# One-hots for the edge counts of a two-layer graph network: three targets in one VectorE pass, and a narrower first matmul per tile

## The reference

```python
x = layernorm(x + L0(x, edges))   # x1 = relu(x @ W_ah + b), three attention convolutions of 4 heads, W_out
x = layernorm(x + L1(x, edges))   # two attention convolutions, 4 heads of 512 and one of 768
# one convolution:
h = x @ W;  e = leaky_relu(as_n[src] + ad_n[dst], 0.2)
p = exp(e - segment_max(e, dst)[dst])
out = segment_sum((p / segment_sum(p, dst)[dst])[:, None] * h[src], dst) + b
```

## Time and profile before

| | us |
|---|---|
| median of 3 runs | 1948.07 |
| lowest, highest run | 1946.56, 1950.36 |
| the profiled execution, its own time | 1945.85 |
| span of its trace | 1944.2 |
| outside the span (own time less span) | 1.65 |
| first stage, to the next stage's first matmul | 240.88 |

### The profile page before, as it was taken

How to read it: one execution, slowest core, us unless ns; L and a number is a source line. 1 busy time by engine, 2 the same in 40 slices (tenths; PEclk the granted TensorE clock), 3 DMA queues, 4 the chain that set the end, 5 groups by cost and what they waited for, 6 DMA issues and landing times. The chain is left out here.

```text
span 1944.2 us, 30898 instructions
## 1 busy us (share of the span) xinstructions
PE 1848.0 (95%) x11497; PEld 1783.2 (92%) x11497; DVE 1445.9 (74%) x2468; ACT 1033.4 (53%) x1634; POOL 140.8 (7%) x139
## 2 busy tenths in 40 slices
PE   6999899999999999997999999989999999999998
PEld 5777789998999999997999899989999999999998
DVE  7787669998889988983545549557888886356766
ACT  4666622126798898874211232257788875232633
POOL 5011022111000000000011111100000000000000
PEclk9999989999999999998999999999999999999999
DMA  4122144455284444537654476482342406545302
GB/s 125 53 61 67 27 143 124 124 137 137 72 203 103 106 105 102 134 71 188 191 172 143 134 197 184 132 224 75 113 141 66 138 27 179 168 122 129 101 17 80
DMA packets 179273, 234.13 MB, mean 120 GB/s; under 512 B 75943, under 2 KB 151655, under 8 KB 178889
## 3 DMA queue, kind: packets, MB, share of 16 engines
q1 hardware_dynamic: 170407, 202.98, 38.6%
q0 software_dynamic: 7984, 27.24, 4.8%
q10 hardware_dynamic: 748, 2.10, 0.4%
HBM read 167.27 MB, written 65.00 MB: 119 GB/s over the span
## 5 line engine op out<-in xcount | busy, mean ns | idle before, releaser
L1692 PE MATMUL p_o<-p_hi,h_parts 125*128 125x416 f32 (+1 forms) x960 | 282.6, 355 | 8.8 <-DVE z L1611 6.2
L1118 PE MATMUL p_o<-first_room,p 125*125 125x193 f32 x1200 | 201.7, 329 | 5.7 <-ACT res L1000 2.9
L1118 PEld LDWEIGHTS p_o<-first_room,p 125*125 125x125 f32 x1200 | 197.0, 189 | 7.1 <-issue 6.7
L1118 PE MATMUL p_o<-h_in,p 125*125 125x193 f32 x1200 | 199.8, 329 | 2.8 <-ACT res L1000 2.8
L1118 PEld LDWEIGHTS p_o<-h_in,p 125*125 125x125 f32 x1200 | 197.6, 189 | 4.3 <-issue 3.0
L1692 PEld LDWEIGHTS p_o<-p_hi,h_parts 125*128 125x128 f32 x960 | 181.6, 189 | 14.9 <-DVE z L1611 10.2
L761 DVE CUSTOM_DVE_ANT_0 max_junk<-src_row,G 125x1250 bf16<-125x1250 f32 x120 | 184.9, 1612 | 3.2 <-ACT src_row L799 1.6
L865 PE MATMUL p_h<-pw_hi,x1T 128*125 128x384 f32 x720 | 187.1, 341 | 0.0
L1068 DVE TENSOR_TENSOR e<-e 125x1250 f32<-125x1250 f32 x120 | 174.3, 1452 | 17.2 <-ACT e L1030 17.1
L1073 DVE SCALAR_TENSOR_TENSOR p<-e,CT 125x1250 f32<-125x1250 f32 x120 | 175.3, 1461 | 4.6 <-PE p_o L1118 0.4
L1408 PE MATMUL p_h<-pw_hi,x2T 128*125 128x256 f32 (+1 forms) x960 | 173.7, 283 | 0.0
(11 more groups left out here) (270 smaller groups left out, 3920.0 us busy)
## 6 DMA issues: line engine op xcount, KB each, us to landing
f_raw<-turned SPq DMA_DIRECT2D x40, 500.0 KB, 9.0
h_parts<-h_rows SPq DMA_DIRECT2D x40, 448.0 KB
turned<-tail_room SPq DMA_DIRECT2D x18, 625.0 KB, 7.3
G<-turned SPq DMA_DIRECT2D x20, 562.5 KB
h_rows<-tail_room SPq DMA_DIRECT2D x22, 424.4 KB
h_rows<-h_out SPq DMA_DIRECT2D x16, 560.0 KB
h_rows<-tail_room SPq DMA_DIRECT2D x14, 560.0 KB
first_room<-in_w_gat POOLq DMA_DIRECT2D x36, 192.0 KB, 2.7
```

Source lines behind the costliest of these rows:

```text
L1118: last = nc.tensor.matmul(p_o[:, b, n * 256:n * 256 + C0 + 1], p[:, g % RING, d * T:(d + 1) * T], h_in[hh][:, s, 0:C0 + 1], start=(s == 0 ...
L1692: last = nc.tensor.matmul(p_o[:, bank(n, c), 0:w], h[:, s, kind, cols].bitcast(F32R), pp[:, g % RING, 0:w], start=(s == 0 and j == 0), sto ...
```

## The change

VectorE makes the target one-hots of slots 0, 1 and 2 by one `tensor_tensor` over 3 x 125 columns: `node_no` repeated three times against the three edge targets, each repeated 125 times (these are F32, `node_no` is I16, the output BF16). The wait ahead of it is for slot 2's buffers of the run before; slots 0 to 2 of `src_hot` then have no wait of their own, slot 3 keeps its own. ScalarE makes the target one-hot of slot 3 alone, so `apart` has one buffer. TensorE opens each bank with the diagonal's columns alone, which lie in one bank or two (126 in all, with an even start and width), and a bank without any of them with two columns; the slice of `band` is now at a constant place.

```diff
-        BY_DVE = RUN // 2
+        BY_DVE = RUN - 1
...
             def one_hots(t, first, count, before):
                 with dve.Fori(0, count) as j:
+                    at = bass.ds(first + j, 1)
+                    dve.wait_ge(hot_free, (before + j) * RUN + BY_DVE)
+                    v.tensor_tensor(dst_hot[:, 0:BY_DVE, :],
+                                    node_no[:, bass.ds(t * T, T)].rearrange("p (o n) -> p o n", o=1).broadcast_to([T, BY_DVE, T]),
+                                    edge_col[:, 1, 0:BY_DVE, at].broadcast_to([T, BY_DVE, T]), ALU.is_equal)
                     for h in range(RUN):
-
-                        dve.wait_ge(hot_free, (before + j) * RUN + (h + 1))
-                        at = bass.ds(first + j, 1)
-                        hot = v.tensor_scalar(src_hot[:, h, :], node_no[:], edge_col[:, 0, h, at], None, ALU.is_equal)
-                        if h < BY_DVE:
-                            hot = v.tensor_scalar(dst_hot[:, h, :], node_no[:, bass.ds(t * T, T)], edge_col[:, 1, h, at],
-                                                  None, ALU.is_equal)
-                        hot.then_inc(hot_ready, 1)
+                        if h >= BY_DVE:
+                            dve.wait_ge(hot_free, (before + j) * RUN + (h + 1))
+                        v.tensor_scalar(src_hot[:, h, :], node_no[:], edge_col[:, 0, h, at], None, ALU.is_equal).then_inc(hot_ready, 1)
...
                 for i, (a, w) in enumerate(CH):
-                    nc.tensor.matmul(p_count[:, i, 0:w], ident_b, band[:, bass.ds(t * -T + (N - T + a), w)],
+                    lo, hi = max(a, t * T), min(a + w, (t + 1) * T)
+                    lo, hi = (lo - a - (lo - a) % 2, hi - a + (hi - a) % 2) if lo < hi else (0, 2)
+                    nc.tensor.matmul(p_count[:, i, lo:hi], ident_b, band[:, N - T + a + lo - t * T:N - T + a + hi - t * T],
                                      start=True, stop=False, skip_group_check=True)
```

## The result

| | before | after |
|---|---|---|
| median, us | 1948.88 (4 runs, 1946.56 to 1950.36) | 1965.6 (4 runs, 1962.13 to 1969.5) |
| ratio after / before | | 1.0094, 95% interval 1.0077 to 1.0112 |
| profiled execution, its span | 1944.2 | 1960.4 |
| first matmul of the next stage | 240.88 | 260.23 |

The kernel became 16.7 us slower; 22.4 had been forecast. The first stage lost 19.35 us, and the later stages took 3 less in this execution.

The account below looks back on a forecast made before the run. TensorE was taken to bound the first stage, with VectorE level; 27.0 - 3.4 - 1.4 + 1.2 - 1.0 = +22.4 us gave a median of 1970.5. Forecast proper 1964 to 1977 (0.70), wider range 1960 to 1981 (about 0.83).

Parts of the forecast that it names:

- The added wait and its row: Between count runs, TensorE waits for VectorE's pass and a source one-hot: 3.05 us a run against 2.15, 0.90 more.
- Thirty passages: Run-to-run passages that pay 0.90 us: 19 in tiles 1 to 4, 6 and 8, 11 in tiles 5, 7, 9; +27.0 us.
- what ScalarE gives back: ScalarE's wait moves to slot 3: 0.57 us in six tiles, -3.4; the late tiles 5, 7, 9 gain 0.47 each, -1.4.
- the free first passage: In tiles 1 to 4, 6 and 8 the first passage costs nothing, as TensorE waits for ScalarE in the first run anyway.
- the four paid ones: In tile 5 VectorE itself comes late, so every passage counts: four at 0.90 us.
- The opening at nothing: Narrower opening of each tile costed at nothing, covered by waits for ScalarE or VectorE; uncovered it would be 2.2 us.
- The end of a tile: The low part of x, on which turn_x waits, comes 0.3 us later in tiles 2, 4, 6 and 8: +1.2 us.
- Tile 0: GpSimd holds VectorE up here; fewer instructions a run, yet passages cost too: -1 us, between -3 and +2.
- The sum: All terms of the first stage together: 27.0 - 3.4 - 1.4 + 1.2 - 1.0 = +22.4 us.
- The faster one: Rival: the passages between runs don't bind, as VectorE keeps its lead; about -8 us, 1940; chance 0.05.
- The clock didn't fall between the runs: Rival: TensorE's pause every run lowers its clock; all thirty at half clock +48 us, a quarter +12; chance 0.05.
- A cheap or dear pass: Two rivals on VectorE's pass: cheap or passages partly covered, 1950 to 1964, chance 0.12; dear, 1977 to 1984, chance 0.08.

Follow-up runs that it names:

- pass_later: The changed kernel with the source one-hots of slots 0 and 1 put ahead of the pass, which then releases both slots; 1950.9 us (one run).
- pass_of_two: The changed kernel with the pass covering slots 0 and 1 only and ScalarE making two target one-hots; 1955.86 us (one run).
- pass_two_sets: The changed kernel with VectorE's target one-hots alternating between two sets of buffers, the single pass kept; 1940.93 us (one run).
- three_apart: The changed kernel with VectorE's three target one-hots made one by one, each slot with its own wait; 1939.1 us (one run).
- pass_old_open: The changed kernel with the wide opening of all 1250 columns back; 1973.11 us (one run; the kernel before took 1952.63 on that chip).
- regs_vector: The kernel before, with VectorE's register loads for both tiles of a step moved ahead of the step's first count; 1940.62 us (one run).
- open_only: The kernel before with the narrower opening alone; 1951.27 us (12 runs) against 1946.84 (18 runs), ratio 1.0019.

## Why the prediction was right, and where it was off

- **The added wait and its row.** Right: 3.05 us a run forecast, 3.05 measured; the pass lasts 0.551 us (0.55 forecast) and leads its successor by 0.47 (0.45 by the scaling from the two-tensor rows, taken as 0.47). `pass_later` and `pass_of_two` change one term each and come out at 2.57 (2.59 expected) and 2.38 (2.39); `pass_two_sets` and `three_apart` take the wait away, and the loss with it.
- **Thirty passages, and what ScalarE gives back.** Right. From opening to close tiles 1 to 9 became longer by 21.9 us in sum; 27.0 - 3.4 - 1.4 = 22.2 was forecast. Tile 1 shows the free first passage (+2.12, of 3 x 0.90 - 0.57 = 2.13), tile 5 the four paid ones (+3.13, of 4 x 0.90 - 0.47 = 3.13).
- **The opening at nothing.** Right inside the changed kernel (`pass_old_open`), where TensorE is busy with slot 2 a slot longer before it waits. Alone the narrow opening costs 0.19%, and its profiles show the loss in tiles with stretches at half clock. I had weighed the clock only against the pauses between runs, not against the wait at a tile's start.
- **The end of a tile.** Wrong, also in sign: +1.2 us forecast, about -3.85 measured (from the close of the even tile to the opening of the next, tile 0's included: 0.57, 0.81, 0.82, 0.82 and 0.83 less).
```profile
73.38 1.00 DVE L283 TENSOR_SCALAR src_hot<-node_no,edge_col 125x1250 bf16<-125x1250 int16 x2
75.76 1.26 DVE L295 TENSOR_TENSOR xT_lo<-p_x,xT_hi 128x500 fp32r<-128x500 f32 x2 [1.38 <-issue]
```

```profile
77.75 1.91 DVE L287 TENSOR_SCALAR src_hot<-node_no,edge_col 125x1250 bf16<-125x1250 int16 x4
79.94 1.26 DVE L295 TENSOR_TENSOR xT_lo<-p_x,xT_hi 128x500 fp32r<-128x500 f32 x2 [0.29 <-issue]
```

  And the source view of the loads there (DVEq is VectorE's sequencer), the first and the last instruction of the three loads, before and after:

```profile
L272 DVEq TENSOR_LOAD <-range_i x1: 311/311/311, 73.9 to 73.9; - x1
L274 DVEq SEQ_ASSERT  x1: 23/23/23, 75.7 to 75.7; - x1
```

```profile
L272 DVEq TENSOR_LOAD <-range_i x1: 312/312/312, 78.1 to 78.1; - x1
L274 DVEq SEQ_ASSERT  x1: 23/23/23, 79.9 to 79.9; - x1
```

  Before, the last source one-hot starts at 73.84 (73.38 + 0.46) and the loads at 73.9. They end at 75.7, the low part follows at 75.76, and the engine has stood idle for 1.38. In the changed kernel the loads run from 78.1 to 79.9, nearly all under the one-hots, which last until 79.66, and the low part follows 0.29 us behind these. `regs_vector` gets the gain without the pass (4.6 us at the five places), and `three_apart`, which has the slot's wait back right ahead of the last one-hot, loses it again.
- **Tile 0.** Forecast -1 between -3 and +2, measured +1.35 (1.16 in the tile, 0.19 before it). Fewer instructions between GpSimd's did not pay, as the pass is held up as well: it lasts up to 1.625 us in the source view, against a median of 0.551. The two long ones start during a two-tensor operation of GpSimd (at 12.17 in 11.84 to 13.38, at 18.54 in 17.78 to 19.44) and both end 0.41 after it. The Trainium skill, "SBUF — State Buffer", section "SBUF: two separate sides", says that VectorE and GpSimd share a pair of ports which one instruction holds for its whole length, and counts a VectorE operation with two SBUF inputs among those that need it, when the GpSimd instruction reads SBUF; these rows agree. How much of the 1.35 is that and how much the clock, which falls differently in each execution (18.7 to 20.6 us for the same tile of the same kernel), stays open.
- **The sum.** 22.2 + 1.2 - 1.0 = 22.4 forecast, 21.9 - 3.85 + 1.35 = 19.4 in the stage. It is 3.0 less because the end of the tiles was 5.05 off and tile 0 2.35 the other way, so that part of the agreement is luck. The median's 16.7 has scatter of the later stages in it.
- **The rivals.** The faster one is excluded: in tiles 1 to 9 no passage but the six free ones went without its wait. The clock didn't fall between the runs: the row from 46 to 55 us has 1.00 with TensorE busy for 6.89 of 9.00 us. The Trainium skill, "TensorE: Matmul & The Clock Gate", section "A second HAM failure mode: psum-queue depth-cycling", reports a kernel whose clock swung because of short pauses between groups of matmuls. Read as a rule, that would have had it fall here too, and the trace does not agree. Half clock did follow some of the longer pauses of `pass_of_two` and `open_only`, though. A cheap or dear pass: neither, 0.47.

## What to carry to other kernels

One instruction that writes several buffers of a ring waits for the last of them to come free; if everything behind it in its queue feeds the same consumer, the lead of the whole ring is lost. Before merging, write down the row from the consumer's last use to its next input and compare it with what the consumer still has in hand: here 1.6 us against 0.7. And look at what stands between the last wait of a loop and the next work on the path: register loads there may be moved ahead, which here ended the waits behind them.

## What the runs showed that I had not expected

- Waits of 1.8 us at the start of an even tile left the clock at 1.00 in the kernel before; 2.1 us in the same place, with an opening 0.3 us shorter, were followed by half clock in seven of twelve cases in three executions, up to 2.9 us lost in one tile (tile 6, 15.40 to 18.32).
- VectorE's three register loads before a loop take 1.8 to 1.9 us of its sequencer and start only after the last wait ahead of them, while queued work goes on; with them out of the way the kernel before gained 4.6 us at five places in one execution.
- A VectorE operation on 375 columns with one I16 operand and one F32 operand repeated from a single column lasts 0.551 us, as an F32 operation of that length would by the rows of 500 and 1250 columns (0.547, an estimate from 0.676 and 1.452); 250 columns last 0.42.
